# A macaron block with a sparse feed-forward: the low parts of the expert weights change engine, and the second half's router moves some steps later

## The reference

```
x = x + 0.5 * ffn(layernorm(x))
x = x + attention(layernorm(x))      # 8 heads of 16, 2 key heads, window of 32 tokens
x = x + 0.5 * ffn(layernorm(x))

ffn(x):  logits = x @ gate_w.T ; the two best of 8 experts per token, their softmax weights scaled to 1
         out = sum over those two of w * (gelu(x @ W1[e] + b1[e]) @ W2[e] + b2[e])
             + gelu(x @ sW1 + sb1) @ sW2 + sb2            # the shared expert, for every token
```

## Time and profile before

| | |
|---|---|
| median of 3 runs | 384.98 us (384.1 to 386.81) |
| the profiled execution's own time | 384.56 us |
| its span | 382.8 us |
| busy: TensorE, VectorE, ScalarE, GpSimd | 317.3, 170.6, 244.5, 211.3 us |
| of GpSimd: indirect DMAs of 92 gathers and 92 returns | 90.2 and 91.3 us |

### The profile page before, as it was taken

One profiled execution on the slowest core, in us unless ns is written; L12 is line 12 of the kernel. 1 busy time (PEld: TensorE's weight loads), 2 busy tenths in 40 slices (PEclk: granted clock), 3 DMA queues, 4 the chain that ended last, 5 costly groups with the idle time before them and its releaser, 6 DMA issues.

```text
span 382.8 us, 10771 instructions
## 1 busy us (share of the span) xinstructions
PE 317.3 (83%) x3591; PEld 271.2 (71%) x3599; DVE 170.6 (45%) x615; ACT 244.5 (64%) x674; POOL 211.3 (55%) x228
## 2 busy tenths in 40 slices
PE   0676597999955898999895799999999689979991
PEld 0355486998844667889784677899888488969881
DVE  6879627100006269755576465854548320000005
ACT  4694265788742885967642578897775258848640
POOL 5263766777774877206334777554353477776510
PEclk9999598999997999999898799999999989989997
DMA  5892544565417153302125424333221746553131
GB/s 167 256 256 70 199 144 147 167 184 172 166 50 282 58 171 89 111 3 78 57 73 192 127 85 158 119 98 112 86 78 41 278 138 195 190 162 104 42 118 55
DMA packets 39222, 50.51 MB, mean 132 GB/s; under 512 B 5803, under 2 KB 23296, under 8 KB 39170
## 3 DMA queue, kind: packets, MB, share of 16 engines
q1 hardware_dynamic: 33192, 37.73, 29.0%
q0 software_dynamic: 5888, 12.07, 12.1%
q10 hardware_dynamic: 90, 0.03, 0.0%
HBM read 16.32 MB, written 9.18 MB: 67 GB/s over the span
## 4 chain that ended last, share of the span: by engine, by line
PE 45%; POOL 17%; issue 12%; DVE 11%; ACT 8%; DMA 6%; SPq 0%; DVEq 0%; ACTq 0%; POOLq 0%
PE y L625 14%; POOL xg L497 10%; POOL yd L505 6%; PE z L589 4%; PE y L640 3%; PE m L807 3%; PE z L591 3%; PE z L590 3%; DMA xg<-xr,from_row 3%; ACT h L883 2%; PE y L628 2%; DVE x L1220 2%; PE m L795 2%; PE m L660 1%; DMA x<-in_L_attn_x_dram 1%
## 5 line engine op out<-in xcount | busy, mean ns | idle before, releaser
L883 ACT ACTIVATE h<-z,w_tile 128x128 f32<-128x128 f32 x368 | 105.1, 373 | 38.1 <-PE z L591 36.0
L505 POOL DMA_INDIRECT yd<-ysb,to_row x92 | 91.3, 992 | 60.3 <-ACT ysb L896 40.0
L497 POOL DMA_INDIRECT xg<-xr,from_row x92 | 90.2, 980 | 49.7 <-issue 41.4
L625 PE MATMUL y<-w,h 128*128 x736 | 105.4, 288 | 0.0
L625 PEld LDWEIGHTS y<-w,h 128*128 128x128 f32 x736 | 93.4, 198 | 1.5 <-issue 0.2
L589 PE MATMUL z<-xgt,w_tile 128*128 128x128 f16 x368 | 71.3, 229 | 13.2 <-ACT xgt L941 6.6
L591 PE MATMUL z<-xgt,w_tile 128*128 128x128 f16 x368 | 71.1, 228 | 0.0
L590 PE MATMUL z<-xgt,w_tile 128*128 128x128 f16 x368 | 71.0, 228 | 0.0
L589 PEld LDWEIGHTS z<-xgt,w_tile 128*128 128x128 f16 x368 | 37.3, 101 | 20.5 <-issue 8.5
L941 ACT ACTIVATE xgt<-m 128x512 f16<-128x512 f16 (+1 forms) x48 | 27.2, 589 | 22.7 <-PE m L686 22.6
L1120 DVE SCALAR_TENSOR_TENSOR x<-y,x 128x512 f32<-128x512 f32 x8 | 5.5, 690 | 76.4 <-PE y L645 76.4
(11 more groups left out here) (198 smaller groups left out, 485.2 us busy)
## 6 DMA issues: line engine op xcount, KB each, us to landing
w_tile<-w SPq DMA_DIRECT2D x92, 258.0 KB
stage<-yd SPq DMA_DIRECT2D x8, 512.0 KB, 4.5
stage<-in_L_ffn_W_dram SPq DMA_DIRECT2D x8, 256.0 KB, 4.5
xr<-xs SPq DMA_DIRECT2D x8, 256.0 KB, 4.2
w<-in_L_ffn_W_dram SPq DMA_DIRECT2D x8, 256.0 KB, 5.3
xg<-xr,from_row POOLq DMA_INDIRECT x92, 3.5
yd<-ysb,to_row POOLq DMA_INDIRECT x92, 2.5
x<-in_L_attn_x_dram SPq DMA_DIRECT2D x4, 256.0 KB, 4.3
```

Of the source, the lines that this page charges most:

```text
L497: pool.indirect_dma_start(out=xg[:, r % XR, :], out_offset=None, in_=xr[ph], in_offset=bass.IndirectOffsetOnAxis(ap=from_row[:, ph, i:i + ...
L505: pool.indirect_dma_start(out=yd[ph], out_offset=bass.IndirectOffsetOnAxis(ap=to_row[:, ph, i:i + 1], axis=0), in_=ysb[:, r % YR, :], in_o ...
L625: pe.matmul(to, h32[:, u % HB, c * P:(c + 1) * P], w2[:, bass.ds(e, 1), c, :].rearrange("p a d -> p (a d)"), start=(c == 0), stop=False, s ...
L883: op = act.activation(h32[:, u % HB, cols], z[:, u % 2, cols], ACT.Gelu, bias=bias[:, c:c + 1], scale=1 / WS)
```

## The change

Most edits are of order and place, one is of an operation:

- The low parts are no longer made by GpSimd but by VectorE, in one operation that scales and subtracts (as the shared expert's was already). ScalarE's scaled float32 copies go away; its eight high parts stay, as `hi_w`, two a step in steps 0 to 3.
- VectorE's step 0 is now `gap 0`, low part 0, `place 0`, `tiles 0`, low part 1, `final 0`, low parts 2 to 7; in step 1 come the low parts of the last two token groups (`lo 2`, `lo 3`), which were in steps 0 and 4.
- TensorE does `pos 0` in the first half of step 1 (before: the second half of step 2) and `idx 0` in step 6 (before: 7).
- The second half's router goes from steps 1 to 13 to steps 9 to 14, `rows 1` of SyncE from step 4 to 10, `turn_w` and `w_hi` from 7 to 12, `masks` from 7 to 20.
- VectorE's `shift` of the last token group stands ahead of `pick_experts(0)` instead of behind it.
- SyncE issues the loads of the eight W1 ahead of the biases' two stores, instead of behind them.

```diff
 PE_AT = {
-    ('tr', 1, 0): 1.01, ('tr', 1, 1): 1.015, ('pos', 0): 2.51, ('tr', 1, 2): 5.51, ('tr', 1, 3): 5.515,
-    ('idx', 0): 7.51, ('logits', 1): 7.52, ('turn_w',): 7.53, ('xtr', 0, 0): 7.54, ('xtr', 0, 1): 8.51,
-    ('xtr', 0, 2): 9.51, ('xtr', 0, 3): 13.51, ('pos', 1): 13.52, ('xtr', 0, 4): 13.53, ('xtr', 0, 5): 13.54,
+    ('pos', 0): 1.01, ('idx', 0): 6.51, ('xtr', 0, 0): 7.54, ('xtr', 0, 1): 8.51, ('xtr', 0, 2): 9.51,
+    ('tr', 1, 0): 9.53, ('tr', 1, 1): 9.535, ('tr', 1, 2): 10.51, ('tr', 1, 3): 10.515, ('logits', 1): 11.51,
+    ('turn_w',): 12.51, ('xtr', 0, 3): 13.51, ('xtr', 0, 4): 13.53, ('xtr', 0, 5): 13.54, ('pos', 1): 14.51,
...
 ACT_AT = {
-    ('tanh', 0): 3.01, ('w_hi',): 7.01, ('xevict', 0, 0): 7.02, ('xevict', 0, 1): 8.01, ('tanh', 1): 9.01,
...
+    ('hi_w', 0): 0.8, ('hi_w', 1): 0.81, ('hi_w', 2): 1.8, ('hi_w', 3): 1.81, ('hi_w', 4): 2.8, ('hi_w', 5): 2.81,
+    ('tanh', 0): 3.01, ('hi_w', 6): 3.8, ('hi_w', 7): 3.81, ('xevict', 0, 0): 7.02, ('xevict', 0, 1): 8.01,
+    ('xevict', 0, 2): 9.02, ('w_hi',): 12.6, ('xevict', 0, 3): 13.51, ('xevict', 0, 4): 13.52,
+    ('xevict', 0, 5): 13.53, ('tanh', 1): 14.6, ('xevict', 0, 6): 18.01, ('xevict', 0, 7): 20.01,
...
 DVE_AT = {
-    ('lo', 2): 0, ('evict', 1, 0): 2.68, ('evict', 1, 1): 2.685, ('gap', 0): 3.16, ('lo', 3): 4, ('place', 0): 4.45,
-    ('tiles', 0): 7.31, ('final', 0): 7.42, ('evict', 1, 2): 7.48, ('evict', 1, 3): 7.485, ('wo',): 7.56,
-    ('masks',): 7.6, ('pick', 1): 7.94, ('gates', 0): 9.01, ('gap', 1): 9.1, ('w_lo',): 9.74, ('gates', 1): 10.43,
-    ('place', 1): 13.86, ('tiles', 1): 17.58, ('final', 1): 19.73, ('comb', 0, 0): 33.93, ('comb', 0, 1): 34.73,
...
+    ('gap', 0): 0, ('w1_lo', 0): 0.1, ('place', 0): 0.2, ('tiles', 0): 0.3, ('w1_lo', 1): 0.35, ('final', 0): 0.4,
+    ('w1_lo', 2): 0.54, ('w1_lo', 3): 0.56, ('w1_lo', 4): 0.58, ('w1_lo', 5): 0.6, ('w1_lo', 6): 0.62,
+    ('w1_lo', 7): 0.64, ('lo', 2): 1, ('lo', 3): 1.05, ('wo',): 6, ('gates', 0): 7, ('evict', 1, 0): 9.6,
+    ('evict', 1, 1): 9.605, ('evict', 1, 2): 10.6, ('evict', 1, 3): 10.605, ('pick', 1): 11.6, ('gap', 1): 11.7,
+    ('w_lo',): 12.7, ('place', 1): 14.7, ('gates', 1): 14.9, ('tiles', 1): 17.58, ('final', 1): 19.73,
+    ('masks',): 20.5, ('comb', 0, 0): 33.93, ('comb', 0, 1): 34.73, ('att_stats', 0): 35.75, ('att_stats', 1): 36.47,
...
 SP_AT = {
-    ('attention',): 0, ('rows', 1): 4, ('load_y', 0): 34, ('rows', 2): 52, ('load_y', 1): 57, ('rows', 3): 81,
+    ('attention',): 0, ('rows', 1): 10, ('load_y', 0): 34, ('rows', 2): 52, ('load_y', 1): 57, ('rows', 3): 81,
...
-SPLIT_HI_AT = {e: e // 2 for e in range(8)}
...
             load_w2(SHARED)
-            store_biases()
             for e in range(E):
                 load_w1(e)
+            store_biases()
             load_biases()
...
-            def split_lo(e):
-                pool.wait_ge(w_scaled, e + 1)
-                pool.tensor_tensor(w1_part(e, 1), w1_raw[:, e].rearrange("p (c f) -> p c f", f=P), w1_part(e, 0),
-                                   ALU.subtract).then_inc(w1_split, 1)
...
-                act.activation(w1_part(e, 0), w1_raw[:, e].rearrange("p (c f) -> p c f", f=P), ACT.Copy, scale=WS)
-                act.activation(w1_raw[:, e], w1_raw[:, e], ACT.Copy, scale=WS).then_inc(w_scaled, 1)
+                act.activation(w1_part(e, 0), w1_raw[:, e].rearrange("p (c f) -> p c f", f=P), ACT.Copy, scale=WS)\
+                    .then_inc(w1_hi_done, 1)
...
+            def split_lo(e):
+                dve.wait_ge(w1_hi_done, e + 1)
+                dve.scalar_tensor_tensor(w1_part(e, 1), w1_raw[:, e].rearrange("p (c f) -> p c f", f=P), WS, w1_part(e, 0),
+                                         ALU.mult, ALU.subtract).then_inc(w1_split, 1)
...
             split_shared_lo()
+            shift("pre", 3)
             pick_experts(0)
-            shift("pre", 3)
```

More of the change, by code:

```diff
@@ L100 @@
[L100 to L113, removed]
-DVE_AT = {
-    ('lo', 2): 0, ('evict', 1, 0): 2.68, ('evict', 1, 1): 2.685, ('gap', 0): 3.16, ('lo', 3): 4, ('place', 0): 4.45,
-    ('tiles', 0): 7.31, ('final', 0): 7.42, ('evict', 1, 2): 7.48, ('evict', 1, 3): 7.485, ('wo',): 7.56,
-    ('masks',): 7.6, ('pick', 1): 7.94, ('gates', 0): 9.01, ('gap', 1): 9.1, ('w_lo',): 9.74, ('gates', 1): 10.43,
-    ('place', 1): 13.86, ('tiles', 1): 17.58, ('final', 1): 19.73, ('comb', 0, 0): 33.93, ('comb', 0, 1): 34.73,
[L119 to L125, removed]
-    ('gates', 2): 59.46, ('tiles', 2): 59.53, ('final', 2): 60.31, ('comb', 1, 0): 60.73, ('att_stats', 2): 61.43,
-    ('att_shift', 2): 62.55, ('comb', 1, 1): 63.66, ('att_lo', 2): 64.2, ('att_stats', 3): 64.35,
-    ('att_shift', 3): 64.98, ('vals', 2): 65.13, ('split', 2): 66.02, ('att_lo', 3): 67.22, ('smax', 2, 0): 68.08,
-    ('split', 3): 69.56, ('smax', 2, 1): 70.66, ('vals', 3): 72.1, ('smax', 3, 0): 72.53, ('smax', 3, 1): 73.15,
-    ('pv_norm', 2, 0): 74.59, ('pv_norm', 2, 1): 76, ('pv_norm', 3, 0): 76.51, ('xadd', 2): 76.78,
-    ('stats', 6): 76.91, ('pv_norm', 3, 1): 77.79, ('shift', 6): 78.28, ('xadd', 3): 79.06, ('lo', 6): 79.23,
-    ('stats', 7): 79.4, ('evict', 3, 0): 79.77, ('evict', 3, 1): 79.775, ('shift', 7): 80.17, ('lo', 7): 81.52,
-    ('evict', 3, 2): 82.09, ('evict', 3, 3): 82.095, ('pick', 3): 83.13, ('gap', 3): 84.44, ('place', 3): 85.15,
-    ('gates', 3): 89.37, ('tiles', 3): 89.45, ('final', 3): 90.14, ('comb', 2, 0): 91.67, ('comb', 2, 1): 95.54,
-    ('comb', 3, 0): 131, ('comb', 3, 1): 131.2,}
@@ new lines @@
+DVE_AT = {
+    ('gap', 0): 0, ('w1_lo', 0): 0.1, ('place', 0): 0.2, ('tiles', 0): 0.3, ('w1_lo', 1): 0.35, ('final', 0): 0.4,
[4 more added lines that the diff above has]
+    ('masks',): 20.5, ('comb', 0, 0): 33.93, ('comb', 0, 1): 34.73, ('att_stats', 0): 35.75, ('att_stats', 1): 36.47,
+    ('att_shift', 0): 37.24, ('att_shift', 1): 38.35, ('att_lo', 0): 38.98, ('split', 0): 40.61, ('att_lo', 1): 42,
+    ('vals', 0): 42.1, ('smax', 0, 0): 42.62, ('split', 1): 43.14, ('smax', 0, 1): 44.26, ('vals', 1): 45.13,
+    ('smax', 1, 0): 45.53, ('smax', 1, 1): 46.03, ('pv_norm', 0, 0): 46.35, ('pv_norm', 0, 1): 46.77,
+    ('pv_norm', 1, 0): 46.89, ('xadd', 0): 47.07, ('stats', 4): 47.27, ('pv_norm', 1, 1): 47.79, ('shift', 4): 48.28,
+    ('xadd', 1): 49.13, ('lo', 4): 49.5, ('stats', 5): 49.86, ('evict', 2, 0): 50.51, ('evict', 2, 1): 50.515,
+    ('shift', 5): 50.83, ('lo', 5): 52.08, ('evict', 2, 2): 52.6, ('evict', 2, 3): 52.605, ('pick', 2): 53.13,
+    ('gap', 2): 54.49, ('place', 2): 55.24, ('gates', 2): 59.46, ('tiles', 2): 59.53, ('final', 2): 60.31,
+    ('comb', 1, 0): 60.73, ('att_stats', 2): 61.43, ('att_shift', 2): 62.55, ('comb', 1, 1): 63.66,
+    ('att_lo', 2): 64.2, ('att_stats', 3): 64.35, ('att_shift', 3): 64.98, ('vals', 2): 65.13, ('split', 2): 66.02,
+    ('att_lo', 3): 67.22, ('smax', 2, 0): 68.08, ('split', 3): 69.56, ('smax', 2, 1): 70.66, ('vals', 3): 72.1,
+    ('smax', 3, 0): 72.53, ('smax', 3, 1): 73.15, ('pv_norm', 2, 0): 74.59, ('pv_norm', 2, 1): 76,
+    ('pv_norm', 3, 0): 76.51, ('xadd', 2): 76.78, ('stats', 6): 76.91, ('pv_norm', 3, 1): 77.79, ('shift', 6): 78.28,
+    ('xadd', 3): 79.06, ('lo', 6): 79.23, ('stats', 7): 79.4, ('evict', 3, 0): 79.77, ('evict', 3, 1): 79.775,
+    ('shift', 7): 80.17, ('lo', 7): 81.52, ('evict', 3, 2): 82.09, ('evict', 3, 3): 82.095, ('pick', 3): 83.13,
+    ('gap', 3): 84.44, ('place', 3): 85.15, ('gates', 3): 89.37, ('tiles', 3): 89.45, ('final', 3): 90.14,
+    ('comb', 2, 0): 91.67, ('comb', 2, 1): 95.54, ('comb', 3, 0): 131, ('comb', 3, 1): 131.2,}
@@ L560, in _ @@
             inv_std("pre", 3)
-            for e in range(E):
-                split_lo(e)
             for n in range(NSTEP + 1):
@@ L1051, in _ @@
                     rows_out(UNIT_AT[n - LAG])
-                for e, at in SPLIT_HI_AT.items():
-                    if at == n:
-                        split_hi(e)
                 extras(n, 1)
```

26 lines of the change are left out of this document (21 added, 5 removed).

## The result

The changed kernel takes 375.91 us (median of 4 runs, 374.08 to 376.44); the kernel before, run beside it, takes 385.89 (384.1 to 388.63). The ratio is 0.973, with an interval of 0.969 to 0.976: 2.7% faster, or some 10 us, where 8.8 were forecast. Ratios leave out executions more than 1.5% above the fastest of their kernel, which concerns three of the seven runs of one experiment and nothing else here. The profiled execution of the changed kernel is the one of 374.08, with a span of 372.3.

The account below looks back on a forecast made before the run. GpSimd was taken to pace the kernel from its first return. Row numbers at 29.16, first product at 37.1 and return at 45.7 (54.47 before) gain 8.8: 384.56 - 8.8 = 375.8, or 376.2 against the median; likeliest range 374 to 378.

Parts of the forecast that it names:

- Selection to row numbers: Router of the first half: selection at 17.69, `place 0` taking 7.37 (12 if slow), row numbers at 29.16 against 38.29.
- The rule for two inputs: Skill-page rule: a VectorE instruction with two SBUF inputs and a GpSimd instruction reading SBUF contend, one blocking the other whole.
- its reading of why the place was late before: Start of `place_pairs` at 24.25 instead of behind the selection: TensorE did `pos 0` behind a step of shared-expert products.
- The two covers: Before the row numbers: ScalarE's high part done by 18.2 for 18.9; TensorE ready for `idx 0` by about 27, else up to 1.5.
- Weights: Before the first routed product: six low parts to 33.2, SyncE's answer at 34.1, landing 3.0, product at 37.1 (36.3 to 40.1).
- that rival: Six low parts on VectorE beside GpSimd's gathers are held, costing 7.9 more: 384 us; chance 0.06.
- First product to first return: First tile: 9.61 as before, less 1.6 for ScalarE's stand at `tanh 1`, plus 0.6 for eight transposes: return at 45.7.
- the granted clock of 0.50 stays in the sum: TensorE at the first tile: stands before it in both orders, so the half clock of 40 to 41 us stays counted.
- Steps 10 to 14: TensorE gets some 2 us of added work where it had stood for tile 11: -1.0 to +2.0, taken as 0.
- TensorE didn't become the bound: Rival for steps 9 to 14: added 2 us show in full plus a late tile 11, 378 to 379.5; chance 0.10.
- SyncE's queue: Rival: biases' load waits for stores behind W1, past 16.6; 379.5 to 382, chance 0.13; slower than before, 389 or more, 0.03.
- Behind the first return: Rest of the kernel: GpSimd's queue has no slack, so the first return's gain of 8.8 goes through to the end.

Follow-up runs that it names:

- second profile of the change: The changed kernel run again unchanged, against the kernel before: 376.25 us, ratio 0.975; its profile is of the execution of 380.01.

## Why the prediction was right, and where its terms were off

**Selection to row numbers: right.** 29.16 forecast, 28.69 measured. `place_pairs` took 7.11, by the distance of the second half (7.37) and not by that of the first (11.91), and the run with GpSimd's subtractions shows why the slow form existed: 13.35. Of the 6.24 between, 5.45 are in operations with one tensor input (`at_lane` 3.66, the cast and the remainder of the slots 0.88 and 0.91), the rest in operations with two. The Trainium skill's page "SBUF — State Buffer", section "Who interferes with whom", also says that `copy`, `cast` and `tensor_scalar` can enter a mode in which VectorE takes the ports that it shares with GpSimd, and that the later of the two is then blocked. The 16 `at_lane` operations, which are `tensor_scalar`, agree with that, 2.69 alone and 6.35 beside subtractions; whether they ran in such a mode no run shows. The rule for two inputs that the prediction drew on covers the smaller part only. Less exact was its reading of why the place was late before: of the 4.79 from 19.46 to 24.25 the step of `pos 0` accounts for 1.0, while the late `shift` held TensorE's shared products until 20.80 (18.11 in the change). Low parts cost 0.60 to 0.62 each by distance, not 0.68.

**The two covers: right, and both needed.** The first high part was forecast to end at 18.2 for a request at 18.9; ScalarE's two high parts ran from 17.58 for 1.14, so the first ended near 18.15, and VectorE began low part 0 at 18.86 without a wait. Moving `shift` back took the cover away at the price of 2.32 that the prediction's numbers imply, plus the lateness of `idx 0`. That second condition was named too (`idx` by about 27, up to 1.5 if late): it ran at 26.80, as soon as its input was there, and in the run with `shift` back it cost the row numbers 1.52 more (4.06 late, 2.54 of them from the start of the place at 22.00).

**Weights: right.** Six low parts ended at 32.54 (33.2 forecast), SyncE's copy went out at 33.52, landed after 2.79 (3.0 forecast, between bounds of 2.2 and 6.0), and released the first product at 36.45 (37.1). Low parts were not held by gathers: 0.62 each, so that rival falls. The second gather paid a little instead, 1.28 for 0.95; the first took 1.54 with low parts beside it, and as long beside VectorE's other operations where the low parts stood ahead of the place.

**First product to first return: the one term that was wrong, by 0.8.** Forecast were 9.61 - 1.6 + 0.6 = 8.6; measured are 45.85 - 36.45 = 9.40. ScalarE's stand at `tanh 1` is gone as said. But "the granted clock of 0.50 stays in the sum" was not so: before, the clock was back to full 3.2 us behind the first product (44.86 to 48.08, where the products go from 0.31 to the 0.22 of the row below), now the second tile still pays 0.31 at 39.92, and the third starts 6.87 behind the first (before: 5.48). With the clock at 1.00 the same distance is 7.96 (37.16 to 45.12), bounded by GpSimd's gathers. And the run with the router early has the stand again and the same first return. So the move of the second half's router to steps 9 to 14 is worth nothing measurable beyond what the other place tried behind `place_pairs` gives; what it costs ahead of it, with the low parts on VectorE and `shift` moved, was not run. It was luck that the sum came out within 0.15 of the measured 45.85: the first product came 0.65 early (0.47 by the row numbers, 0.21 by the landing), and that hid this term's error.

```profile
48.08 0.22 PE L589 MATMUL z<-xgt,w_tile 128*128 128x128 f16 x1
```

**Steps 10 to 14: right.** Taken at 0 between -1.0 and +2.0; the fifth return is 8.97 earlier against 8.62 for the first, so -0.35. TensorE didn't become the bound.

**SyncE's queue: the rival was real, its price too small to count.** The second store was issued at 9.78 and the load that waits for both at 14.95; W1's issues had ended at 8.54, and their data took 6.2 us to land by the median. Issued ahead of W1, the stores held up nothing: that load went out at 14.59, straight behind W1's last issue. The Trainium skill's page "DMA: Bandwidth & Descriptors", section "Queues, rings and completion order", says that each DMA engine consumes descriptors in ring order. That the stores landed only about when W1 did agrees with it. The load was issued 0.94 later than in the earlier trace rows, W2's issue then took 5.62 us (before: 8.04), as the prediction had held against this rival, and the queue stood free at 27.98, 5.5 us before it was wanted.

**Behind the first return: as forecast, and then more, which is open in part.** In the two profiles the shift stays between 8.25 and 8.97 up to the 43rd return. Then it grows to 9.98 at the 46th and to 10.46 at the last. GpSimd's return rows show where the largest piece comes from. Before:

```profile
186.62 0.97 POOL L505 DMA_INDIRECT yd<-ysb,to_row  x1 [0.30 <-issue]
191.56 0.97 POOL L505 DMA_INDIRECT yd<-ysb,to_row  x1 [3.97 <-ACT ysb L896]
```

After:

```profile
178.17 0.97 POOL L506 DMA_INDIRECT yd<-ysb,to_row  x1 [0.30 <-issue]
181.71 1.02 POOL L506 DMA_INDIRECT yd<-ysb,to_row  x1 [2.57 <-ACT ysb L890]
```

The wait for ScalarE is 1.40 shorter (2.57 for 3.97), and the stretches around it differ in the granted clock. Before, and then after:

```profile
188.00:190.00 2.00, 2.00 (x15) 2.00 (x13) 1.90 (x5) 1.08 (x4) 0.00 (x0) 0.50 0.10 33
```

```profile
180.00:182.00 2.00, 2.00 (x16) 1.55 (x16) 1.86 (x6) 1.56 (x6) 0.29 (x1) 1.00 0.00 0
```

TensorE had stood for 0.8 and 0.3 us ahead of both and was granted 0.50 in one execution and 1.00 in the other. In the second profile of the change, with the same stands, it was granted 0.50 there again, the wait for ScalarE is 3.79, and the shift against the kernel before is down to 7.3 at the 46th return. So this piece belongs to the execution and not to the order; what decides it in one execution stays open. But the medians of two groups of runs put the change 9.98 and 9.87 ahead of the kernel before, some 1.3 more than the shift of the first return. Whether part of that is the change's own work behind the first return, or the scatter of the runs, one profile of the kernel before can't show. And the time forecast, 376.2, lies nearer to the measured 375.91 than the gain does (8.8 and 9.98), since the kernel before ran 0.9 above the 384.98 that the forecast started from.
